# Opening of a gated two-layer kernel: when the fourth context matrix is loaded, and in which steps its two parts are taken

## The reference, cut to what matters

```python
def _L0_xattn_ref(hidden_states, token_ids, Wg, Wu, Wd):   # called with ctx_2048 as Wg, Wu and Wd
    E, VOCAB = 4, 25000
    tid = jnp.clip(token_ids, 0, VOCAB - 1)
    expert_ids = jnp.minimum(tid // (VOCAB // E), E - 1)
    out = jnp.zeros_like(hidden_states)
    for e in range(E):
        g = jax.nn.silu(jnp.einsum('bsd,fd->bsf', hidden_states, Wg[e]))
        u = jnp.einsum('bsd,fd->bsf', hidden_states, Wu[e])
        y = jnp.einsum('bsf,df->bsd', g * u, Wd[e])
        out = jnp.where((expert_ids == e)[..., None], y, out)
    return out
...
x = x + jnp.tanh(g_xattn[0]) * _L0_xattn_ref(_layernorm(x, axis=-1), itok, ctx_2048, ctx_2048, ctx_2048)
x = x + jnp.tanh(g_ffn[0]) * _L0_ffn_ref(_layernorm(x, axis=-1), input_ids, gate_w, gate_b, W1, W3, W2, Ws1, Ws3, Ws2)
```

## Time and profile before

| | us |
|---|---|
| median of 3 runs | 491.08 |
| lowest and highest | 490.11, 491.33 |
| the profiled execution, its own time | 491.09 |
| its span in the profile | 489.3 |
| TensorE matmul busy | 465.7 (95%) |
| VectorE busy | 329.2 (67%) |
| ScalarE busy | 257.8 (53%) |

### The profile page before, as it was taken

The page is one execution under the profiler, slowest core; times in us unless marked ns, Lnnn a source line. Parts: engine busy times, 40 slices in busy tenths (PEclk is TensorE's granted clock), DMA queues, the critical chain, the costliest instruction groups (busy, mean ns, idle before and its releaser), DMA issues.

```text
span 489.3 us, 7789 instructions
## 1 busy us (share of the span) xinstructions
PE 465.7 (95%) x2493; PEld 393.7 (80%) x2493; DVE 329.2 (67%) x723; ACT 257.8 (53%) x379; POOL 208.7 (43%) x175
## 2 busy tenths in 40 slices
PE   2879999999999989999999999999999999999994
PEld 1458877878888867888888989999989999888983
DVE  6559988998886833378747786666666666666520
ACT  4834543545553433472344576666666666666531
POOL 0602434655444354452456624343336544432232
PEclk9989999999999998999999999999999999999998
DMA  7826545666665443261649999998969999997545
GB/s 286 286 72 234 176 153 172 217 222 219 228 207 201 150 112 134 70 80 24 79 104 222 248 314 292 254 256 241 265 228 241 280 259 276 257 246 225 109 56 74
DMA packets 29164, 95.02 MB, mean 194 GB/s; under 512 B 4816, under 2 KB 5328, under 8 KB 28624
## 3 DMA queue, kind: packets, MB, share of 16 engines
q0 software_dynamic: 17040, 43.66, 36.2%
q1 hardware_dynamic: 11808, 50.98, 31.7%
q10 hardware_dynamic: 288, 0.01, 0.0%
HBM read 67.50 MB, written 28.70 MB: 197 GB/s over the span
## 4 chain that ended last, share of the span: by engine, by line
PE 85%; DVE 7%; DMA 2%; issue 2%; another core or an unknown queue 1%; POOL 1%; ACT 1%; POOLq 0%; DVEq 0%
PE psG L1278 46%; PE psY L1278 29%; PE psT L1283 6%; DMA ys<-in_x,idx 2%; PE psG L1523 1%; DMA tok_i<-in_ids 1%; DVE arena L1060 1%; DVE xh_sb L906 1%; PE psY L1295 1%; DVE arena L915 1%; DVE arena L911 1%; DVE stats L940 0%; DVE stats L933 0%; DVE gu L922 0%
## 5 line engine op out<-in xcount | busy, mean ns | idle before, releaser
L1278 PE MATMUL psY<-arena 128*128 (+2 forms) x372 | 94.4, 401 | 0.0
L1278 PEld LDWEIGHTS psY<-arena 128*128 128x128 f32 (+1 forms) x372 | 67.5, 188 | 13.3
L504 POOL DMA_INDIRECT ht<-out,idx x32 | 34.6, 1080 | 72.1 <-PE psT L1283 56.3
L1278 PE MATMUL psG<-arena 128*128 x228 | 59.0, 408 | 4.4 <-DVE arena L915 4.4
L1278 PE MATMUL psY<-slot,arena 128*128 128x512 f32 (+1 forms) x240 | 61.1, 399 | 0.0
L1053 DVE TENSOR_TENSOR slot<-raw,slot 128x1536 fp32r<-128x1536 f32 x25 | 43.8, 1756 | 23.8 <-ACT slot L628 21.9
L1053 DVE TENSOR_TENSOR arena<-raw,arena 128x1536 fp32r<-128x1536 f32 x24 | 42.1, 1756 | 22.9 <-ACT arena L628 22.3
L1278 PEld LDWEIGHTS psG<-arena 128*128 128x128 f32 x228 | 42.7, 193 | 14.7 <-issue 6.2
L1278 PE MATMUL psG<-arena,slot 128*128 128x512 f32 x216 | 52.7, 400 | 0.0
L1278 PEld LDWEIGHTS psY<-slot,arena 128*128 128x128 f32 (+1 forms) x240 | 43.7, 188 | 9.0 <-ACT xh_sb L672 0.3
L1278 PEld LDWEIGHTS psG<-arena,slot 128*128 128x128 f32 x216 | 41.1, 193 | 8.5
(11 more groups left out here) (227 smaller groups left out, 807.0 us busy)
## 6 DMA issues: line engine op xcount, KB each, us to landing
raw<-in_w SPq DMA_DIRECT2D x51, 768.0 KB
padded<-xh_sb SPq DMA_DIRECT2D x19, 256.0 KB
raw<-in_ctx_t SPq DMA_DIRECT2D x2, 1024.0 KB, 8.8
ht<-in_ctx_t SPq DMA_DIRECT2D x1, 1024.0 KB, 11.7
xh_sb<-in_ctx_t SPq DMA_DIRECT2D x1, 1024.0 KB
out<-log_sb SPq DMA_DIRECT2D x4, 256.0 KB
ht<-out,idx POOLq DMA_INDIRECT x32
xb<-in_x,idx POOLq DMA_INDIRECT x19
```

Of the source, the lines that this page charges most:

```text
L504: pool.indirect_dma_start(ht[:, n, :], None, halves_of_out, slots(e * NA + a, 0)).then_inc(g_here[n], 16)
L1278: ins = pe.matmul(ps, left[a], right[b], start=n == 0 and m == 0, stop=n == total - 1 and m == 2)
```

## The change

Three things move. SyncE waits for the landing of the third gather (tile 2, `xa_here[2]`) before it issues the load of context 3, in place of `first_out`; the bias and the four stores of zeros stand behind that wait too. ScalarE takes the high part of context 3 in step 1, before that step's SiLU, where it took it in step -1. VectorE takes the two halves of the low part in steps 1 and 2, where it took them in steps 0 and 1; the first half now waits for its own end (`link`), since step 2's L906 overwrites that half of `xh_sb`, and behind the second half VectorE waits until `ctx_lo_done` is 4, for the same reason.

```diff
@@ sync
-            sp.wait_ge(first_out, 1)
+            sp.wait_ge(xa_here[2], 16)
             sp.dma_start(ctx_raw(E1 - 1), ctx_t[E1 - 1, :, :]).then_inc(ctx_here[E1 - 1], 16)
             sp.dma_start(bias_b[:, :], gate_b).then_inc(in_bias, 16)
             sp.wait_ge(zeroed, 1)
@@ scalar, step
                 if have(known, -1):
                     act.wait_ge(gT_ps, t)
                     act.activation(gT[0], psT[1][:, :], ACT.Copy).then_inc(gT_hi, 1)
+                if known == 1:
+                    high_ctx(3)
                 if known == NT:
...
-                if known == -1:
-                    high_ctx(3)
                 if known in (-1, 0):
                     take_rest(2, known + 3)
@@ vector, step
                 if have(known, 1) and known not in (FIRST + 1, 0):
                     low_h()
-                if known in (0, 1):
-                    if known:
+                if known in (1, 2):
+                    if known == 2:
                         dve.wait_ge(ctx_lo_done, 3)
-                    i = low_ctx(3, known, 2)
-                    if known:
-                        i.then_inc(ctx_lo_done, 1)
+                        low_ctx(3, 1, 2).then_inc(ctx_lo_done, 1)
+
+                        dve.wait_ge(ctx_lo_done, E1)
+                    else:
+                        link(low_ctx(3, 0, 2))
```

## The result

The changed kernel took 492.28 us (median of 20 runs, 490.68 to 496.03), the kernel before on the same chip 490.86 (20 runs). The ratio is 1.0034, with a 95% interval of 1.0020 to 1.0048. So it is slower, by 1.4 us in the medians and 1.7 by the ratio, where 1.1 us less was forecast, and it lies outside the range given (486.5 to 491.8). The profiled execution took 493.31, with a span of 491.5 where before had 489.3.

A forecast was written before the change was run, and what follows sets the result against it. Bound by tile 2's gather into `ys` waiting behind context 3, then by TensorE's lowered clock. Terms -3.75 - 1.6 + 1.0 + 3.25 = -1.1 took 491.1 to 490.0 us; range 486.5 to 491.8, the forecast's own 488.8 to 490.8.

The forecast's parts named there:

- What bounds: At the start, tile 2's gather waits behind context 3, costing almost 4 us; TensorE's lowered clock is the second loss.
- Term 1: Start: the third gather lands at 18.8, so TensorE's first psG product starts at 23.36, 3.75 us earlier.
- Term 2: TensorE's first psG product: the clock stays high, so 4.61 us becomes 3.00, -1.6 us.
- Term 3: ScalarE, step 1: context 3's high part fits the idle time before the SiLU but for 0.1; 0 to +0.1 us.
- Term 4: VectorE, steps 0 to 2: step 2 gains a 1.22 us piece, so +1.0 us; L906 of step 4 ready at 48.7.
- Term 5: L906 of step 4 waits for store and scatter behind the later weight loads, until 51.95: +3.25 us.
- lower bound: Earliest landing of tile 0's store, for L906 of step 4: 7.8 us behind the first load's issue, at 50.0.
- upper bound: Latest start of L906 of step 4, with a further gather of 0.26 MB mixed in: 52.6.
- second clock drop: TensorE, step 4: a new gap of about 2 us lowers the clock, about 0.5 us; part of a rival at 0.09.
- No stall at the weight loads: L906 of step 4: store and scatter land before 48.7, so no wait; -4.35 us, time 486.7; chance 0.17.
- slower rival: Start: the third gather still takes 6.5 us, TensorE idles 2 us and the clock falls; +1.9, time 493.0; chance 0.13.
- page's rule: DMA queues before L906 of step 4: by turns the scatter lands by about 47, only the store holds; time some 489.

The follow-up runs named there:

- control with early loads: The kernel before with its three weight loads let go one context earlier (`ctx_lo_done` at 3, not 4): 485.55 us, ratio 0.9995.
- third set: The changed kernel with all three weight loads left in place, then two, then one, the others let go early: 493.32, 490.05, 487.84 us against 490.91.
- first set: Runs on the loads' place; the one cited is the changed kernel with tile 0's store issued ahead of the three weight loads: 490.86 us, ratio 0.9972.
- two loads late: The changed kernel with the first weight load let go one context earlier and the other two left in place: 490.05 us, ratio 0.9979.
- cure: The changed kernel with all three weight loads let go one context earlier (`ctx_lo_done` at 3, not 4): 481.0 us against 485.94, ratio 0.9900.
- loads spread: The changed kernel with the three weight loads issued one each ahead of the stores of tiles 2, 3 and 4: 489.9 us, ratio 0.9951.
- one late: The changed kernel with the first two weight loads let go one context earlier and one left in place: 487.84 us, ratio 0.9936.
- parts only: The changed kernel with SyncE's wait put back to `first_out`, so only context 3's high and low parts are moved: 498.82 us, ratio 1.0155.

## Why the prediction was wrong, by its own steps

**What bounds.** Right: the gather of tile 2 behind context 3, then the clock.

**Term 1, the start.** The mechanism was right, the size was 3.07 for 3.75 us. The third gather took 3.8 us from its issue, where 3.6 was expected, but was issued at 17.22 and not at 15.19, because the issue ahead of it took 3.00 us. That does not undo the reading of the 8.88 us. In the control with early loads, in which context 3 goes out as early as before, the third gather was issued at 17.10 too and still landed at 24.0:

```profile
17.10 6.92 DMA ys<-in_x,idx
```

With context 3 ahead of it the landing stays where it was, whenever the gather is issued; without it the gather lands 3.6 to 4.9 us behind its issue, at 18.7 to 21.0, in the profiles of the runs here. Nor is the late issue all of the shortfall. In the third set's profile of the same changed kernel the third gather was issued at 15.24 and landed by 20.1, and the first product still started at 23.83, because L915 then waited 0.58 us for ScalarE's high part of tile 0, which ended at 22.8 and not at 22.34.

**Term 2, the clock.** Right: 1.6 us, with PEclk at 1.00 from 20 to 40.

**Term 3, ScalarE.** Right at the margin. Context 3 landed 9.1 us behind its issue, not 6, at 30.1; ScalarE came to it at 30.3. The change has no slack there.

**Term 4, VectorE.** +1.0 was forecast; 49.2 ready against 53.07 - 4.7 = 48.4 gives +0.8. Right.

**Term 5, the loads ahead of the store.** This is the step that failed. Its mechanism was right: the store's queue, the scatter, both behind the loads, and L906 of step 4 waiting for them; the first and third set show each part of it. Its size was not. Forecast was 9.8 us from the first load's issue to L906, and a wait of 3.25; measured were 13.65 and 7.2. Two things in the sum were off, and together they are the 3.8 us. The bytes: the 9.6 us of before stood for 3.27 MB, but 4.14 had moved by 55, for three gathers and tile 1's store were in front of the landing; at before's own 0.34 MB/us they are 2.6 us. And the end: 0.2 us was allowed behind the bulk, and 1.4 passed from 55 to L906 at 56.42, most of it the tail in which the DMA engines were nearly idle. The rate that was carried over was right on the mean, 340 GB/s and 339, in spite of the 311 in 45 to 48; only the lower bound used the 423. The upper bound given, 52.6, added one gather, and three gathers and a store came. What makes the tail is not settled here: it is in both profiles of the changed kernel and not in that with two loads late.

**What was left out.** The second clock drop was named, at 0.5 us, in a rival; it came, at 0.8. TensorE's idle stretch was 6.08 us and not 2, but that its length set the price isn't shown. That the kernel before loses about as much to a drop near 185, and the changed kernel in its profile not, was not in the prediction at all. Had before not had it, the changed kernel would be some 3 us behind in the medians (1.4 and 1.6), an estimate that takes the one profile of before for all its executions.

**The rivals.** No stall at the weight loads (486.7, so 4.4 us below before) is what the cure reaches: 4.9 below. The slower rival was the wrong one: it put the loss in the gather, which landed early enough, and that its 493.0 lies near the measured 492.3 is luck. Of the page's rule that DMA engines take turns between queues with work (the Trainium skill, "DMA: Bandwidth & Descriptors", section "Queues, rings and completion order"), the runs show the half. From 48 on both queues moved in the changed kernel; but from 45 to 47.5 q0 moved nothing, with the scatter issued at 42.85, and with the store out of the way (first set) the scatter still took until 51.1, 8.9 us from its issue, so turns did not bring it through by 47.

## What to carry to other kernels

Moving the last piece of a group also moves everything that is gated on the group being whole. Ask of each such wait what it truly needs: here the loads needed two contexts and waited for four. And price a transfer that becomes ready beside a bulk load by what all queues will have moved by its landing, the next step's traffic included, at the mean rate of a like stretch, and leave room for its last packets.

## What the runs showed of the hardware

GpSimd's issue of an indirect DMA, 0.95 us as a rule, takes 1.9 to 3.1 us where a VectorE piece with two SBUF operands (2.29 us, fp32) overlaps it. If the piece starts ahead of the second gather's issue, that one takes 3.0 to 3.1; if behind it, the third takes 1.9 to 2.4. Both orders are in profiles of the same changed kernel: the piece started at 13.76 in one and at 14.51 in the other. When the piece was moved, the long issue moved with it, and each long issue ends 0.8 to 0.9 us behind the piece. The Trainium skill, "SBUF — State Buffer", section "SBUF: two separate sides", describes a port pair which VectorE and GpSimd hold in turn and exclusively, and says that GpSimd can't write DMA descriptors while it is locked out. For GpSimd the traces agree; VectorE they don't show held up: the piece took the same 2.29 us where an issue had begun first (13.90 against 13.94 in the kernel before).

A wait of nearly the same length cost a clock drop near 185 in some profiles and none in others. TensorE's wait there ended in a drop after 2.35 us (before), 2.40 (two late) and 2.52 (loads spread), and in none after 2.28 (one late), 2.41 (changed) and 2.49 (parts only). Where it came between before and the changed kernel it was worth 1.6 us, about as much as the whole difference of the medians. What decides it is open. Where two kernels differ by 0.3%, one profile each is not enough to say where the time went far behind the change; the medians and the stages next to the change are.
